# Cross-attention maxima from 32-row score tiles with four masked key copies, split into halves and partly issued among the transposed scores

## The reference

```python
x = x + _L0_attn_ref(_layernorm(x, axis=-1), Wq, Wk)
x = x + _L0_xattn_ref(_layernorm(x, axis=-1), ctx, ctx, Wq, bq, Wk, bk, Wv, bv, Wo)
x = x + _L0_ffn_ref(_layernorm(x, axis=-1), ...)
# cross-attention: B = 128 sequences, N = M = 64 positions, 16 heads of 8
scores = einsum('bhnd,bhmd->bhnm', q, k) * 8 ** -0.5
weights = softmax(scores, axis=-1)
out = einsum('bhnm,bhmd->bhnd', weights, v)          # then out @ Wo.T
```

## Time and profile before

| | |
|---|---|
| runs (3) | median 498.4 us, 498.06 to 499.16 |
| the profiled execution | 494.99 us, of it 493.1 us between the first and the last instruction |
| TensorE matmul / weight load | 459.2 us (93%) / 317.0 us (64%) |
| VectorE | 407.9 us (83%) |
| ScalarE | 378.0 us (77%) |
| GpSimd | 302.1 us (61%) |
| granted TensorE clock | 0.998 of full speed |

### The profile page before, as it was taken

The page is one execution under the profiler, slowest core; times in us unless marked ns, Lnnn a source line. Parts: engine busy times, 40 slices in busy tenths (PEclk is TensorE's granted clock), DMA queues, the critical chain, the costliest instruction groups (busy, mean ns, idle before and its releaser), DMA issues.

```text
span 493.1 us, 21697 instructions
## 1 busy us (share of the span) xinstructions
PE 459.2 (93%) x8758; PEld 317.0 (64%) x8758; DVE 407.9 (83%) x1105; ACT 378.0 (77%) x563; POOL 302.1 (61%) x393
## 2 busy tenths in 40 slices
PE   7999998998889999999997869999999998999996
PEld 6777776654456666666665545555555655788885
DVE  6888658979588888888888798889898865999896
ACT  4888766898888888898897468888889677755550
POOL 5454224775699898899828646799999852013000
PEclk9999999999999999999999999999999999999999
DMA  6486459530011010110111011232323223276543
GB/s 202 112 201 180 124 146 245 160 108 1 3 37 37 27 46 29 27 50 27 28 47 48 3 44 58 100 112 89 122 82 119 86 84 113 74 227 217 186 144 78
DMA packets 51806, 47.11 MB, mean 96 GB/s; under 512 B 13200, under 2 KB 39952, under 8 KB 51728
## 3 DMA queue, kind: packets, MB, share of 16 engines
q1 hardware_dynamic: 51440, 45.90, 31.4%
q10 hardware_dynamic: 288, 0.13, 0.1%
HBM read 29.76 MB, written 15.99 MB: 93 GB/s over the span
## 4 chain that ended last, share of the span: by engine, by line
PE 41%; POOL 15%; DVE 9%; issue 7%; ACT 3%; POOLq 0%; DVEq 0%; ACTq 0%
PE ps L1684 7%; PE ps L1587 7%; PE ps L882 4%; PE ps L956 3%; PE ps L853 3%; POOL v_or_front L1064 3%; DVE c_mx L655 3%; PE ps L902 3%; PE ps L1484 2%; PE ps L1213 2%; POOL e_inv_root L1093 2%; POOL e_scaled L1375 2%; POOL e_inv_root L1078 2%; PE ps L980 2%; POOL k_or_hidden L1383 2%
## 5 line engine op out<-in xcount | busy, mean ns | idle before, releaser
L598 POOL TENSOR_TENSOR copies_or_layer<-k_or_hidden,w_mask 128x512 bf16<-128x512 f32 x93 | 97.4, 1072 | 3.6 <-DVE c_work L686 2.6
L655 DVE TENSOR_REDUCE c_mx<-ps 128x16 f32<-128x1024 f32 x64 | 78.3, 1224 | 22.6 <-PE ps L853 22.5
L756 ACT ACTIVATE c_work<-ps 128x2048 f32<-128x2048 f32 x32 | 60.1, 1878 | 7.8 <-PE ps L882 7.8
L1560 ACT ACTIVATE copies_or_layer<-k_or_hidden 32x512 f32 (+1 forms) x64 | 40.2, 628 | 23.1 <-PE ps L1587 22.5
L1375 POOL TENSOR_TENSOR e_scaled<-e_raw,e_rden 128x512 f32<-128x512 f32 x16 | 20.8, 1300 | 43.5 <-DMA e_rden<-dispatch_inverses 43.5
L766 ACT ACTIVATE c_q_bd<-x_all,w_mask 128x512 f32<-128x512 f32 x64 | 45.5, 714 | 0.0
L1573 DVE TENSOR_TENSOR o_slot_out<-ps,w_b 128x512 f32<-128x512 f32 x64 | 41.1, 686 | 5.1 <-PE ps L1587 4.6
L1426 ACT ACTIVATE e_slot_in<-ps 128x1024 f32<-128x1024 f32 x30 | 30.7, 1023 | 17.2 <-PE ps L1484 17.2
L1484 PE MATMUL ps<-copies_or_layer,v_or_front 64*128 64x256 f32 x256 | 36.0, 399 | 3.1 <-ACT e_slot_in L1426 3.1
L1587 PE MATMUL ps<-w_w,copies_or_layer 64*32 64x128 f32 x2048 | 36.9, 273 | 0.8 <-DVE o_slot_out L1573 0.8
L902 PE MATMUL ps<-c_work,c_v_bd 128*18 128x64 f32 x2048 | 35.1, 220 | 1.9 <-DVE c_o_tok L667 1.8
(11 more groups left out here) (169 smaller groups left out, 1175.4 us busy)
## 6 DMA issues: line engine op xcount, KB each, us to landing
x_all<-x_scratch SPq DMA_DIRECT2D x64, 128.0 KB, 2.9
combine_scratch<-v_or_front SPq DMA_DIRECT2D x14, 512.0 KB, 2.8
ctx_sb<-combine_scratch SPq DMA_DIRECT2D x14, 512.0 KB, 3.3
x_sb<-in_x SPq DMA_DIRECT2D x16, 256.0 KB, 3.4
x_scratch<-a_x SPq DMA_DIRECT2D x16, 256.0 KB, 2.6
ctx_sb<-in_ctx SPq DMA_DIRECT2D x16, 256.0 KB, 3.6
e_rden<-dispatch_inverses SPq DMA_DIRECT2D x64, 64.0 KB, 2.0
out<-o_y SPq DMA_DIRECT2D x30, 128.0 KB, 2.9
```

The lines of the kernel that those rows point to most:

```text
L598: ins = nc.gpsimd.tensor_tensor(k_bd[:, c.m2, s, :], k32[:, c.v, :], w["mask8"][:, s:s + 1].to_broadcast([P, TOK]), ALU.mult)
L655: nc.vector.reduce_max(mx[:, c.m2, :, p], ps[:, SCORE:SCORE + 2, :].rearrange("p a (h m) -> p (a h) m", m=N), AX_X).then_inc(mx_sb.sem, 1)
L756: nc.scalar.activation(prob[:, h, :], ps[:, 0:4, :].rearrange("p a b -> p (a b)"), ACT.Exp, scale=float(HD) ** -0.5).then_inc(p_sb.sem, 1)
```

## The change

The eight masked key copies over 64 rows become four over 32 rows (`mask4`). VectorE makes one a step in place of two, GpSimd three in place of six, ScalarE one in place of three for each chunk of the run-up. A pass of the lead scores is eight matmuls of 32 rows by 256 columns instead of four of 64 by 512. Two row groups of a pass share a PSUM bank, so a pass goes in two halves: `scores` issues row groups 0 and 2 and raises `sc_half`; `scores_end` waits until that half is complete, issues row groups 1 and 3 and releases the maximum. For p0 and p2 both halves are issued inside `scores_T`: the first between the tiles of L882 of row groups 1 and 3 and those of 0 and 2, the second behind them. p1's halves stand ahead of and behind L965, p3's ahead of and behind L980. In the run-up both halves stand together.

In the run-up VectorE now normalises (L686) before it takes the maximum and the next moments (L679), and the last chunk's projection of values and its copy move into step 0. At the border to the dispatch stage, sums, normalisation, unit vectors, moments, squares and maxima of chunks 0 to 3 are put in another order on VectorE, `norms` of chunk 1 moves behind the roots of chunk 3 on GpSimd, ScalarE exchanges `hat_of` of chunk 3 for the square of chunk 2, and TensorE turns tokens and maxima earlier in step 16. In step 0 of `Dispatch.rest` the copies come before the moments, and ScalarE's copy of slots before `hat_of`.

```diff
-    MASK_SLOTS, MASKS_DVE, EARLY = 8, 3, 3
-    EARLY_LEAD = {-16: (0, ()), -15: (0, (3,)), -14: (0, (4,)), -13: (0, (5,)), -12: (0, (6,)), -11: (0, (7,)),
-                  -10: (1, (3,)), -9: (1, (4,)), -8: (1, (5,)), -7: (1, (6,)), -6: (1, (7,)),
-                  -5: (2, (3,)), -4: (2, (4, 5, 6, 7))}
-    EARLY_K = {-13: (0, 0), -12: (0, 1), -11: (0, 2), -9: (1, 0), -8: (1, 1), -7: (1, 2), -4: (2, 0), -3: (2, 1), -2: (2, 2)}
+    MASK_SLOTS, MASKS_DVE, EARLY = 4, 1, 3
+    EARLY_LEAD = {-16: (0, ()), -14: (0, (1,)), -13: (0, (2,)), -12: (0, (3,)), -9: (1, (1,)), -8: (1, (2,)), -7: (1, (3,)),
+                  -5: (2, (1,)), -4: (2, (2, 3))}
+    EARLY_K = {-12: (0, 0), -8: (1, 0), -3: (2, 0)}
...
             elif t.k >= 0:
-                masks_k(t.plus(EARLY), range(MASKS_DVE - 1, MASKS_DVE + 2))
...
                 dispatch.affine(pool, Chunk(None, 1))
-                dispatch.norms(pool, Chunk(None, 1))
                 dispatch.roots(pool, Chunk(None, 3))
                 dispatch.shift_of(pool, Chunk(None, 3))
+                dispatch.norms(pool, Chunk(None, 1))
...
-            if t.k - 1 in EARLY_SCORES:
-                row_max(Chunk(None, EARLY_SCORES[t.k - 1][0]), EARLY_SCORES[t.k - 1][1])
...
+            if t.k - 1 in EARLY_SCORES:
+                row_max(Chunk(None, EARLY_SCORES[t.k - 1][0]), EARLY_SCORES[t.k - 1][1])
...
             if t.k == CHUNKS:
                 dispatch.copies(dve, Chunk(None, 0))
+                dispatch.unit(dve, Chunk(None, 1))
             normalise(t.plus(-1), 0)
             spread_k(t.plus(EARLY), 0)
             row_max(t.plus(2), 0)
+            if t.k == CHUNKS - 1:
+                dispatch.total(dve, Chunk(None, 0))
+                dispatch.normalise(dve, Chunk(None, 1))
+            if t.k == CHUNKS:
+                dispatch.maxima(dve, Chunk(None, 0))
             c = t.plus(-2)
             if c:
...
                 dispatch.unit(dve, Chunk(None, 0))
-                dispatch.square(dve, Chunk(None, 1))
-                dispatch.total(dve, Chunk(None, 1))
-                dispatch.moments(dve, Chunk(None, 3))
-                dispatch.gathered(dve, Chunk(None, 3))
             if t.k == CHUNKS:
-                dispatch.maxima(dve, Chunk(None, 0))
-            spread_k(t.plus(EARLY), 1)
+                dispatch.negate(dve, Chunk(None, 0))
             row_max(t.plus(2), 1)
             row_max(t.plus(2), 2)
             normalise(t.plus(-1), 1)
             if t.k == CHUNKS - 2:
+                dispatch.moments(dve, Chunk(None, 3))
                 dispatch.square(dve, Chunk(None, 0))
-                dispatch.total(dve, Chunk(None, 0))
-                dispatch.normalise(dve, Chunk(None, 1))
             if t.k == CHUNKS - 1:
+                dispatch.gathered(dve, Chunk(None, 3))
                 dispatch.turned(dve, Chunk(None, 0))
-                dispatch.unit(dve, Chunk(None, 1))
+                dispatch.square(dve, Chunk(None, 1))
+                dispatch.total(dve, Chunk(None, 1))
             if t.k == CHUNKS:
...
+        def keep_v(c):
+            act.wait_ge(v_ps.sem, v_ps.at(c))
+            nc.scalar.activation(v_all[:, c.v * PC:(c.v + 1) * PC, :].rearrange("p a d -> p (a d)"), ps[:, v_bank(c), :],
+                                 ACT.Copy).then_inc(v_sb.sem, 1)
...
+                if c.plus(1): keep_v(c)
...
-            if t.k >= 0: spread_q(t.plus(1), 1, 1)
+            if t.k == 0: keep_v(end)
...
-            if t.k == CHUNKS: dispatch.hat_of(act, Chunk(None, 3))
-            if t.k >= 0: spread_q(t.plus(1), 2, 1 if t.k < CHUNKS - 2 else 2)
...
+            for T in (0, 2):
+                score_tiles(c, p, T).then_inc(sc_half.sem, 1)
+
+        def scores_end(c, p):
+            if not c:
+                return
+            pe.wait_ge(sc_half.sem, sc_half.at(c, 2 * p + 2))
+            for T in (1, 3):
+                ins = score_tiles(c, p, T)
+            ins.then_inc(sc_ps.sem, 1)
+
+        def score_tiles(c, p, T):
+            u, a = p // 2, p % 2
             for r in range(2):
-                for T in range(2):
-                    rows, q_at, k_at = slice(64 * T, 64 * (T + 1)), (4 * u + 2 * r + a) * N, (4 * a + 2 * u + r) * N
-                    ins = nc.tensor.matmul(ps[N * r:N * (r + 1), SCORE + T, :].rearrange("p (s m) -> p s m", s=8),
-                                           q_lead[rows, c.m2, q_at:q_at + N], k_bd[rows, c.m2, :, k_at:k_at + N], start=True, stop=True)
-            ins.then_inc(sc_ps.sem, 1)
-
-        def scores_T(c, u):
+                rows, q_at, k_at = slice(32 * T, 32 * (T + 1)), (4 * u + 2 * r + a) * N, (4 * a + 2 * u + r) * N
+                ins = nc.tensor.matmul(ps[N * r:N * (r + 1), SCORE + T // 2, T % 2 * 4 * N:(T % 2 + 1) * 4 * N].rearrange("p (s m) -> p s m", s=4),
...
+        def scores_T(c, u, other=None, p=0):
...
+            for T in range(4):
+                tiles(0, T)
+            for T in (1, 3):
+                tiles(1, T)
+            scores(other, p)
+            for T in (0, 2):
+                ins = tiles(1, T)
             ins.then_inc(st_ps.sem, 1)
+            scores_end(other, p)
...
+                if c.plus(1): project_v(c)
...
             if t.k in EARLY_SCORES:
                 scores(Chunk(None, EARLY_SCORES[t.k][0]), EARLY_SCORES[t.k][1])
-            if t.k < CHUNKS - 1: scores_T(t.plus(0), 0)
-            if t.k >= 0: scores(t.plus(2), 0)
+                scores_end(Chunk(None, EARLY_SCORES[t.k][0]), EARLY_SCORES[t.k][1])
+            if t.k < CHUNKS - 1: scores_T(t.plus(0), 0, t.plus(2), 0)
...
                 if c.plus(-3): pe.wait_ge(x2_sb.sem, x2_sb.at(c.plus(-3)))
                 nc.tensor.transpose(ps[0:PC * HEADS, MISC, 0:P], mx[:, c.m2].rearrange("p h a -> p (h a)"), w["ident"][:]).then_inc(mT_ps.sem, 1)
-            scores_T(t.plus(0), 1)
-            if t.k >= 0: scores(t.plus(2), 2)
+            if t.k >= 0: scores_end(t.plus(2), 1)
+            scores_T(t.plus(0), 1, t.plus(2), 2)
+            if t.k == CHUNKS:
+                dispatch.turn_tokens(pe, Chunk(None, 1))
+                dispatch.turn_maxima(pe, Chunk(None, 0))
             turn(t.plus(-1), 1)
             values(t.plus(0), 0)
             if t.k == CHUNKS - 1: dispatch.turn_tokens(pe, Chunk(None, 0))
-            if t.k == CHUNKS:
-                dispatch.turn_tokens(pe, Chunk(None, 1))
-                dispatch.turn_maxima(pe, Chunk(None, 0))
+            if t.k == CHUNKS: dispatch.shifts(pe, Chunk(None, 0))
             if t.k >= 0: scores(t.plus(2), 3)
...
                 for p in range(PC):
                     ins = nc.tensor.transpose(ps[:, MISC, p * P:(p + 1) * P], o_tok[:, c.m2, p, :], w["ident"][:])
                 ins.then_inc(oT_ps.sem, 1)
+            if t.k >= 0: scores_end(t.plus(2), 3)
             if t.k == CHUNKS - 1:
                 pe.wait_ge(p_sb.sem, p_sb.at(end))
                 dispatch.logits_T(pe, Chunk(None, 0))
-            if t.k == CHUNKS: dispatch.shifts(pe, Chunk(None, 0))
             turn(t.plus(0), 0)
             if t.k == CHUNKS - 1: dispatch.logits(pe, Chunk(None, 0))
...
-                    self.moments(dve, t.plus(5))
-                    self.unit(dve, t.plus(2))
-                    self.copies(dve, t.plus(1))
+                    if t.k:
+                        self.moments(dve, t.plus(5))
+                        self.unit(dve, t.plus(2))
+                        self.copies(dve, t.plus(1))
+                    else:
+                        self.copies(dve, t.plus(1))
+                        self.unit(dve, t.plus(2))
...
-                if t.k >= 0: self.hat_of(act, t.plus(4))
+                if t.k > 0: self.hat_of(act, t.plus(4))
                 if t.plus(1): slots(t.plus(0), 0)
-                c = t.plus(3)
-                if c:
-                    act.wait_ge(self.normed.sem, self.normed.at(c))
-                    if c.plus(-2): act.wait_ge(self.summed.sem, self.summed.at(c.plus(-2)))
-                    nc.scalar.activation(self.junk[:, c.m2], xn[:, c.m4], ACT.Square).then_inc(self.squared.sem, 1)
+                if t.k == 0: self.hat_of(act, t.plus(4))
+                if t.k >= 0: self.square_of(act, t.plus(3))
                 if t.plus(1): slots(t.plus(0), 1)
...
```

More of the change, by code:

```diff
@@ L671, in _ @@
         for t in steps:
+            c = t.plus(LEAD_X + 2)
+            if c:
+                dve.wait_ge(rooted.sem, rooted.at(c))
+                if c.plus(-2): dve.wait_ge(xT_ps.sem, xT_ps.at(c.plus(-2)))
+                for p in range(PC):
+                    ins = nc.vector.tensor_scalar(xn[:, c.m2, p, :], x_tok(c, p), mv[:, c.m2, p, 0:1], rstd[:, c.m2, p:p + 1],
+                                                  ALU.subtract, ALU.mult)
+                ins.then_inc(normed.sem, 1)
             if t.k - 1 in EARLY_SCORES:
@@ L904, in values, with project_v @@
             ins.then_inc(o_ps.sem, 1)
+        def project_v(c):
+            if c.v: pe.wait_ge(v_sb.sem, v_sb.at(c.plus(-1)))
```

(21 more changed lines are left out.)

46 lines of the change are left out of this document (21 added, 25 removed).

## The result

| | before | after |
|---|---|---|
| runs beside each other | 497.8 us, 494.9 to 499.2 (6 runs) | 508.8 us, 508.1 to 512.1 (5 runs) |
| the profiled execution, its span | 495.0, 493.1 | 508.1, 506.3 |
| VectorE / GpSimd, share of the span | 83% / 61% | 79% / 50% |

The ratio is 1.024 (95% interval 1.019 to 1.029): 11 us slower, where 4.5 us had been forecast. A sixth run of the changed kernel took 847.7 us at a granted clock of 1.00; it stands in neither the median nor the ratio, and nothing in its record explains it. The time lies just inside the range and above everything that the likeliest case allowed (507).

The account below looks back on a forecast made before the run. A step was taken as half TensorE, half a ping-pong between matmul and VectorE's maximum. Run-up -0.5, steps +9.5 and hand-over -4.5 gave +4.5 us on a median of 498.4: 502.9 us, range 494.5 to 509.

Parts of the forecast that it names:

- the likeliest case: Whole kernel: the predicted chain of waits holds, time 500.5 to 507 us; chance 0.60.
- the step: Cross-attention's chunk steps: 9.79 us against 8.94, +9.5 us over 12 steps, known to about -0.35 to +0.3 each.
- The mask: VectorE's mask in a step: 0.48 us, its removal worth nothing in the chain since VectorE waits after L709 anyway.
- no slack: Before p1's second half: VectorE allows L965 at 5.22, TensorE brings it at 5.23, so no wait but no slack.
- TensorE's stretch to p1: In a step, from the second L667's end: p0's first half at 2.23 us, p1's first half at 5.00 (4.75 before).
- p2's split: In a step, p2's halves: 0.35 us from first to second half (bounds 0.2 and 0.5), 0.36 more to its maximum.
- The run-up: Before the steps: -2.1 us from normalising first, about -0.9 from moves; with split costs and step 0, sum -0.5.
- The +1.5 for the split in front of step 0: Run-up passes with halves back to back: +0.24 us each, +1.5 for the first six.
- The hand-over: From the last steps into the dispatch stage: -4.5 us from removed waits, bounds -6.5 and -1.
- the 1.30 at the first copies: First dispatch step: copies ahead of moments and scaling remove a TensorE wait of 1.30 us, gaining another 1.3 or so.
- TensorE stays the bound: Rival in the steps: maxima never hold TensorE up, step 8.6 us, time 488.5 us; chance 0.12.
- The half passes do not run beside L882: Rival in the steps: joined tiles take turns, 0.3 to 0.5 us more a step, 507 to 510 us; chance 0.13.

Follow-up runs that it names:

- e9: Changed kernel with GpSimd's three masks of a step moved behind its copies of the values: 508.2 us, ratio 1.022, step 10.15 us.
- e1: Changed kernel with VectorE's one mask moved from ahead of p0's maximum to ahead of p3's: 508.3 us, ratio 1.023, step 10.15 us.
- e4: Changed kernel with both halves of p0 and p2 issued behind all tiles of the transposed scores: 509.2 us, ratio 1.025, step 10.33 us.
- e6: Kernel before with only VectorE's run-up order changed, normalisation ahead of early maximum and statistics: 492.2 us, ratio 0.989.
- e5: Changed kernel with the old scores (eight masks, whole 64-row passes), keeping the new run-up and hand-over: 490.5 us, ratio 0.990.
- e10: Kernel with only the new run-up and hand-over, the dispatch's maxima, their transposes and shifts put back in old places: 486.3 us, ratio 0.977.
- e3: Changed kernel with p3 and p1 whole and VectorE's mask ahead of p3's maximum, joins kept: 502.5 us, ratio 1.012, step 9.73 us.

## Why the prediction was right and where it was not

The direction and the mechanism were right: a step is a ping-pong between halves of passes and maxima, the split lengthens it, and TensorE's shorter stream gives nothing back. What failed is the size of one term, the step: 9.79 forecast, 10.45 measured, a miss of 0.66 where I had allowed 0.3. Its largest part is VectorE's mask, taken at 0.48 and measured at 1.05. The chain laid beside the two traces, times after D (e9 gives the same last column as e1 within 0.02):

| point of the chain | forecast | changed kernel | with the mask moved (e1) |
|---|---|---|---|
| p3's maximum starts | 0.91 | 0.99 | 0.99 |
| p0's first half | 2.23 | 2.37 | 2.37 |
| p0's maximum | 3.31 | 3.84 | 3.31 |
| p1's first half | 5.00 | 5.23 | 5.23 |
| L997 (was L965) | 5.22 | 5.79 | 5.46 |
| p1's second half, maximum | 5.46, 5.82 | 5.99, 6.34 | 5.69, 6.05 |
| p2's first half | 7.14 | 7.62 | 7.33 |
| p2's maximum | 7.85 | 8.49 | 8.20 |
| next D | 9.79 | 10.45 | 10.15 |

- **The mask**, 0.30 of the 0.66. I took L646 at 0.48 from the earlier trace rows; in the new phase it runs into GpSimd's mask each step. It lengthens VectorE's side by 0.53, and of that 0.30 shows (e1, e9), because without it TensorE's own stretch to p1 sets the step. I had written "no slack" for this place and yet called the masks worth nothing; no slack was the half that mattered.
- **TensorE's stretch to p1**, 0.23: p3's second half stands 0.59 behind L1013 and not 0.49, by which p3's maximum is 0.08 late (the change of tiling has its 0.10 there too), p0's first half waits 0.06 longer for that maximum, and from this half to L988 it is 0.76 (221.44 to 222.20) and not 0.66, since the joined second half adds more than the sum had for it.
- **p2's split**, 0.12: the second half is 0.40 behind the first (forecast 0.35) and its maximum 0.47 behind that (forecast 0.36), together 0.16, of which 0.04 comes back from p1's maximum to p2's first half (1.28, forecast 1.32). The bounds of 0.2 and 0.5 held both; the half ends behind L899's last tiles, and unjoined (e4) the way from first half to maximum is 0.12 shorter.
- These are 0.65 of the missing 0.66. Over 12 steps the miss is 7.6 us (17.1 less 9.5); the two ends miss by -2.3 and +2.2 and cancel, and 1.2 lie behind them. That makes 8.7 between the profiled executions, whose difference is 13.1; between the medians it is 11.0, since the profiled execution lay 2.8 below the median of the kernel before and 0.7 below that of the changed one.
- **The run-up** was too small by 2.3: the order alone gave 2.8 (e6), as against 2.1, and the moves 1 to 2. The +1.5 for the split in front of step 0 didn't come: the changed kernel starts step 0 at 128.45, e5 with old passes at 128.25. Step 0 itself cost +1.9, more than the +1.0.
- **The hand-over** was too large by 2.2. The two waits of the earlier trace rows did go (1.66 to 0.26, 2.03 to none; D to D 12.13, now 8.02), and the late p3 of step 13 took its 1.0 (9.65 against 8.66). But a reordered last step brought new waits, 10.76 against 9.25, and the 1.30 at the first copies gave only 0.7. Counting the waits that an order removes and none that it makes was the fault; e10 takes back 0.9 of it in its trace.
- **+1.2 in the dispatch and the last layer** is no larger than what this stretch differs by between kernels with the same code in it: 193.5 us in e9, 193.8 in e10, 194.8 in e3 and 195.0 in the changed kernel; with the old code 193.75 in the kernel before and 195.35 in e6. What moves it stays open.

Of the rivals, "TensorE stays the bound" had its chain right in one respect only. When the placements are mended TensorE does become the bound (e3) but for the 0.14 at p2, and at 9.73: my 8.6 counted tiles and drains and left out that a whole pass holds TensorE 0.3 longer while it waits for its own half. "The half passes do not run beside L882" is partly true: from L899's start to the second half is 1.20 in e3 with no wait for VectorE in between, against 0.87 for L899's own rounds. Yet tiles of both kinds start within 0.02 us of each other there (216.37), so some of it does run side by side; how the 0.33 divides between taking turns, the second half's wait and the order of L899's tiles no run shows. Its price is 0.1 a step, not the 0.3 to 0.5 that I gave it; that the time falls in its interval of 507 to 510 is chance. The wait inside a pass stands there because two row groups of a pass write the same bank; passes without it weren't tried, so that it is needed isn't shown here.

## What to carry to other kernels

An instruction's price is the price in its place. If an edit shifts the phase between two engines, look for the row in which the same instruction was slow (here 22 masks with a mean of 570 ns, most of them at 480 and four from 670 to 1360), and ask whether the new phase makes that the rule. Splitting an operation around a foreign wait makes its second half wait for that engine, and not splitting it makes the engine wait for itself; price both before counting saved columns. And a bundle should be taken apart: here the new scores lost 1.5 us a step, and the reorderings beside them were worth 5 us by themselves and 11 with one of them taken back, the latter in part by the clock.
